# Ten dense pieces in the first filled step, six in the last: a shift by two in a fused two-layer kernel

## The chip, the cores and the metric

The kernel runs on one core of a Trainium2 chip. The metric is the device time of one execution in microseconds (us); less is better. The time before is 886.98 us, the median of three runs (885.87 to 887.53).

## The reference

The reference is two transformer layers on x (32 entries of 64 tokens, 512 features, fp32), each with a condition vector per entry.

```python
# first layer
h = rms(x) * (ln1_w * (1 + cond @ ln1_tw.T))
q, k, v = rope(h @ Wq.T), rope(h @ Wk.T), h @ Wv.T       # 8 heads of 64, one k/v head
x = x + softmax(q @ k.T / 8) @ v @ Wo.T
h = rms(x) * (ln2_w * (1 + cond @ ln2_tw.T))
x = x + (silu(h @ Wg.T) * (h @ Wu.T)) @ Wd.T             # 2048 inner features
# second layer
h = layernorm(x) * (1 + scale(cond)) + shift(cond)
q, c = h @ Wq.T, h @ Wkd.T                                # 16 heads of 32, 4 k/v heads
k, v = c @ Wku.T, c @ Wvu.T
x = x + softmax(mask(rope(q) @ rope(k).T / sqrt(32))) @ v @ Wo.T
```

Attention runs over the 64 tokens of an entry.

## The kernel before, in words

The 2048 tokens are 16 tiles of 128 (two entries each). All matmuls that need fp32 accuracy are made of three: each operand is split into a high part (a cast) and a low part (the difference), and `three` (lines 642 to 645) adds high x high, low x high and high x low. So a weight chunk needs a cast on ScalarE (`guh`, `wdh`) and a subtraction on GpSimd (`gul`, `wdl`) after its DMA.

**The dense part** (gate, up, silu, down of the first layer) is cut into 64 groups: 16 groups of 128 inner features for each of 4 blocks of 512 tokens. Group n has on TensorE (`mlp`, lines 798 to 825) the pieces gate(n), first pair of down(n-1), up(n), second pair of down(n-1). Gate and up are 12 matmuls of 512 columns each, into banks BG and BU; a down pair is two tiles of 3 matmuls, into the two banks BD. Group 0 has two pieces, two come at the end: 256 in all. Every engine has a generator with the same number of pieces (`fill`, line 40, takes the next `count`):

- ScalarE (1698): with gate, silu into `sg` and `wdh`(n); with up, `ah`(n), the cast of `af`; with the second pair, `guh`(n+2) (in group 1 this stands for group 0 too).
- VectorE (1254): with the first pair, two additions of down banks to `xres` (`add_down`, 1252), which free the banks; with up, `af` = up x silu (1265); with the second pair, an addition, `al`(n) = af - ah (1247), an addition.
- GpSimd (518): with gate, `wdl`(n) (516); with the second pair, `gul`(n+2) (511).

TensorE's waits within the pieces: gate(n) for `gul`(n) and for silu(n-1); up(n) for `af`(n-1); a down pair of n for `al`(n), `wdl`(n) and, tile by tile, for the addition that freed its bank (`down`, 786 to 796, the wait at 793).

**The attention part** goes tile by tile, one tile a step, and dense pieces fill TensorE's time. Steps s = 1 to 15 are the first layer's attention, u = -1 to 15 the second's. The order of each engine is written out by hand; the tables `FILL0` and `FILL1` (lines 20, 21) say how many pieces stand at each place of a step. In steps 5 to 15 TensorE does: scores(s), qkv(s+1), fill f1, projection(s-1), fill f2, context(s), fill f3 (lines 1002 to 1028). In u = 0 to 8: scores1(u), f1, qkv1(u+1), projection, f2, f3, context1(u), f4, f5 (1029 to 1062). u = 9 (TAIL) has f1, then qkv1(10), one piece, the transposes of the probabilities, one piece; u = -1 has f1, qkv1(0), projection, f2, f4.

The places of the other engines in steps 6 to 15:

- VectorE (1448 to 1498): softmax_sub(s), turn_x2 of the tile that is made ready for the dense part (steps 6 to 9 and 11 to 14, u = -1 to 2), softmax_norm (it waits for exp), turn_probs, rope_mul(s+1), f1, add_x, turn_queries, f2, low_ctx, scale_h2, f3. In u: softmax_sub1, turn_x2, stats1, two pieces of f1, sums, scaling, turn_probs1, the rest of f1, rope_mul1, and so on.
- ScalarE (1846 to 1889): exp(s), values(s+1), f1, f2, high_ctx, high_h2, square2, high_h, f3, square, norm2 of the next tile (1667; it waits for GpSimd's power). In u also the scale and shift of y (1748), between f4 and f5.
- GpSimd (578 to 611): rstd, rope_sum, f1, f2, low_h2, low_h, f3, rstd2 of the next tile (478).

**Turning through memory.** From step 5 the probabilities (`tp`) are transposed in 32 x 32 blocks on VectorE, written to device memory and read back as `pT` (`probs_away`, `probs_back`, lines 308 to 317); x2, y and the queries go the same way. These DMAs and the loads of the dense weights are all issued by the SP queue, in order, and SP waits in order (397 to 452): in a step x2_away, load_down(n), load_gate_up(n+1), probs_away, x2_back, probs_back, queries_away, queries_back, load_down(n+1), load_gate_up(n+2), load_down(n+2), load_gate_up(n+3), with n = 2 in step 5 and 3 more in each step. load_down(n) waits for `wdl`(n-2) (280), load_gate_up(n) for `gul`(n-2) (274). The context matmuls wait for `pT` (749).

Of the kernel before, what the change touches and what calls it, by code (L numbers as in the profile page):

```python
# [16 lines left out]

FILL0 = {s: (4, 4, 4) for s in range(5, 16)}  # L20
FILL1 = {-1: (4, 4, 0, 4, 0), **{u: (4, 2, 2, 2, 2) for u in range(0, 9)}, 9: (2, 0, 0, 0, 0)}

HEAD, TAIL = 4, 9

# [20 lines left out]
def build(nc, x, xT, pos, condT, ln1_w, ln1_twT, ln2_w, ln2_twT, WqkvT, WoT, gu, WdT,  # L45
# [21 lines left out]
    with ExitStack() as ctx:  # L67
# [153 lines left out]
        def in_layer(t):  # L221
            return 0 <= t < NT
# [237 lines left out]
        def _(pool):  # L460
# [117 lines left out]
            for s in range(1, NT):  # L578
                f1, f2, f3 = FILL0.get(s, (0, 0, 0))
                ready, soon = PREP0.get(s), PREP0.get(s + 1) if s < NT - 1 else PREP1[-1]  # L580
# [31 lines left out]
            for u in range(-1, NT):  # L612
                f1, f2, f3, f4, f5 = FILL1.get(u, (0,) * 5)
                ready, soon = PREP1.get(u), PREP1.get(u + 1)
# [26 lines left out]
        def _(pe):  # L641
# [78 lines left out]
            def scores(t):  # L720
                if t < TURN_Q0:
                    pe.wait_ge(a_qT, t + 1)
                    pe.wait_ge(a_kT, t + 1)
                else:
                    pe.wait_ge(ld_q0, 16 * (t - TURN_Q0 + 1))
                if t > HEAD + 1:
                    pe.wait_ge(a_ch, t)
                    pe.wait_ge(a_cl, t)
                    pe.wait_ge(a_x, t - 1)
                for j in range(KT):  # L730
                    for b in range(2):
                        for i in range(2):
                            r, q = slice(HD0 * i, HD0 * (i + 1)), slice(S * b, S * (b + 1))
                            mm = pe.matmul(ps[q, XB[2 + i], S * j:S * (j + 1)], qkT[r, j, q], qkT[r, KT, q],
                                           start=True, stop=True)
                mm.then_inc(a_sc, 1)
# [265 lines left out]
            for s in range(1, NT):  # L1002
                f1, f2, f3 = FILL0.get(s, (0, 0, 0))
                scores(s)
# [24 lines left out]
            for u in range(-1, NT + 1):  # L1029
                f1, f2, f3, f4, f5 = FILL1.get(u, (0,) * 5)  # L1030
                if in_layer(u):
# [33 lines left out]
        def _(dve):  # L1065
# [382 lines left out]
            for s in range(1, NT):  # L1448
                f1, f2, f3 = FILL0.get(s, (0, 0, 0))
                ready, soon = PREP0.get(s), PREP0.get(s + 1) if s < NT - 1 else PREP1[-1]  # L1450
# [48 lines left out]
            for u in range(-1, NT - 1):  # L1499
                f1, f2, f3, f4, f5 = FILL1.get(u, (0,) * 5)  # L1500
                ready, soon = PREP1.get(u), PREP1.get(u + 1)
# [69 lines left out]
        def _(act):  # L1571
# [274 lines left out]
            for s in range(1, NT):  # L1846
                f1, f2, f3 = FILL0.get(s, (0, 0, 0))
                ready, soon = PREP0.get(s), PREP0.get(s + 1) if s < NT - 1 else PREP1[-1]
# [41 lines left out]
            for u in range(-1, NT - 1):  # L1890
                f1, f2, f3, f4, f5 = FILL1.get(u, (0,) * 5)
                ready, soon = PREP1.get(u), PREP1.get(u + 1)
# [91 lines left out]
```

## Time and profile before

| what | value |
|---|---|
| median of three runs | 886.98 us (885.87 to 887.53) |
| profiled execution | 887.57 us |
| its span (first to last instruction) | 885.7 us |
| TensorE matmuls busy | 852.0 us (96%) |
| TensorE weight loads busy | 707.2 us (80%), beside the matmuls |
| VectorE busy | 631.7 us (71%) |
| ScalarE busy | 447.2 us (50%) |
| GpSimd busy | 406.6 us (46%) |
| mean granted TensorE clock | 0.988 of full |

Busy time is the sum of the instructions of an engine. TensorE is the fullest by far, so a time that TensorE stands idle is paid in full, while idle time of another engine costs only where TensorE waits for it. Times in rows of the timeline are microseconds from the span's start. PE is TensorE, DVE VectorE, ACT ScalarE, POOL GpSimd, SP the queue that issues DMAs.

### The profile page before, as it was taken

The numbers are of one execution on the slowest core, as the hardware profiler recorded it, in microseconds if no ns is written. First come the engines' busy times: TensorE is split into PE (matmuls) and PEld (weight loads), VectorE is DVE, ScalarE is ACT, GpSimd is POOL, SyncE is SP. The second block draws the span as 40 slices with busy tenths as digits, with TensorE's granted clock in tenths as the row PEclk, the third lists the DMA queues.
The fourth block names the chain that finished last, engine by engine and source line by source line (L and its number), as shares of the span: only waits on it lengthen the run. The fifth ranks groups of instructions, "written<-read, shape, count | busy, mean of one in ns | idle before, by whom it ended". The sixth has DMA issues, their size and how long they took to land.

```text
span 885.7 us, 15530 instructions
## 1 busy us (share of the span) xinstructions
PE 852.0 (96%) x5864; PEld 707.2 (80%) x5864; DVE 631.7 (71%) x1005; ACT 447.2 (50%) x821; POOL 406.6 (46%) x304
## 2 busy tenths in 40 slices
PE   9798999999999999999989899999999999999997
PEld 6686888788788888787878678788888888888885
DVE  6686577677666677677546877887877867868886
ACT  4665444544444444445445564563553654644662
POOL 2456445545545545537444644544534534431331
PEclk9899999999999999999999899999999999999999
DMA  9811535435425435334423446355354354330001
GB/s 348 330 32 37 172 99 159 124 110 160 122 87 168 122 104 154 116 99 151 156 96 90 169 122 185 115 166 156 121 164 139 114 175 142 117 102 13 25 27 36
DMA packets 114298, 113.54 MB, mean 128 GB/s; under 512 B 57520, under 2 KB 80048, under 8 KB 114224
## 3 DMA queue, kind: packets, MB, share of 16 engines
q1 hardware_dynamic: 113504, 112.45, 39.8%
q8 instruction: 47, 0.77, 0.4%
q10 hardware_dynamic: 720, 0.09, 0.1%
q14 instruction: 27, 0.22, 0.1%
HBM read 88.15 MB, written 24.38 MB: 127 GB/s over the span
## 4 chain that ended last, share of the span: by engine, by line
PE 65%; DVE 11%; ACT 9%; issue 8%; POOL 6%; POOLq 0%; DVEq 0%; ACTq 0%
PE ps L643 20%; PE ps L645 19%; PE ps L644 19%; PE ps L757 2%; POOL gul L511 2%; ACT yf L1763 1%; PE ps L918 1%; ACT L1643 1%; POOL wdl L516 1%; DVE al L1247 1%; DVE ex L1232 1%; PE ps L689 1%; DVE af L1265 1%; ACT ah L1710 1%; ACT guh L1688 1%
## 5 line engine op out<-in xcount | busy, mean ns | idle before, releaser
L511 POOL TENSOR_TENSOR gul<-rgu,guh 128x1024 fp32r<-128x1024 f32 x64 | 154.3, 2411 | 217.5 <-ACT guh L1688 217.5
L1252 DVE TENSOR_TENSOR xres<-ps,xres 128x512 f32<-128x512 f32 x256 | 174.3, 687 | 67.3 <-PE ps L645 67.3
L643 PE MATMUL ps<-h2h,guh 128*128 128x512 f32 x512 | 205.0, 400 | 2.1 <-issue 2.1
L645 PE MATMUL ps<-h2l,guh 128*128 128x512 f32 x512 | 200.6, 392 | 0.0
L644 PE MATMUL ps<-h2h,gul 128*128 128x512 f32 x512 | 200.2, 391 | 0.0
L643 PE MATMUL ps<-wdh,ah 128*128 128x512 f32 x256 | 102.3, 399 | 14.7 <-DVE al L1247 14.7
L643 PEld LDWEIGHTS ps<-h2h,guh 128*128 128x128 f32 x512 | 96.5, 189 | 23.1 <-issue 2.5
L645 PEld LDWEIGHTS ps<-h2l,guh 128*128 128x128 f32 x512 | 96.5, 188 | 21.1
L1710 ACT CAST ah<-af 128x512 fp32r<-128x512 f32 x64 | 39.8, 621 | 143.8 <-DVE af L1265 138.2
L644 PEld LDWEIGHTS ps<-h2h,gul 128*128 128x128 f32 x512 | 96.5, 189 | 19.6
L644 PE MATMUL ps<-wdh,al 128*128 128x512 f32 x256 | 100.7, 393 | 0.0
L645 PE MATMUL ps<-wdl,ah 128*128 128x512 f32 x256 | 100.7, 393 | 0.0
L516 POOL TENSOR_TENSOR wdl<-rwd,wdh 128x512 fp32r<-128x512 f32 x64 | 82.5, 1289 | 13.4 <-ACT wdh L1696 13.3
L1265 DVE TENSOR_TENSOR af<-ps,sg 128x512 f32<-128x512 f32 x64 | 44.2, 690 | 48.5 <-issue 25.2
L643 PEld LDWEIGHTS ps<-wdh,ah 128*128 128x128 f32 x256 | 48.5, 189 | 30.0 <-DVE al L1247 20.2
L1688 ACT CAST guh<-rgu 128x1024 fp32r<-128x1024 f32 x64 | 66.9, 1045 | 0.0
L1702 ACT ACTIVATE sg<-ps 128x512 f32<-128x512 f32 x64 | 38.2, 597 | 55.4 <-PE ps L645 55.2
L467 POOL TENSOR_TENSOR stat<-stat,minus_half 128x1 f32<-128x1 f32 x48 | 38.3, 798 | 42.2 <-DVE stat L1133 40.9
L645 PEld LDWEIGHTS ps<-wdl,ah 128*128 128x128 f32 x256 | 48.6, 190 | 10.3
L644 PEld LDWEIGHTS ps<-wdh,al 128*128 128x128 f32 x256 | 48.7, 190 | 9.3
L1247 DVE TENSOR_TENSOR al<-af,ah 128x512 fp32r<-128x512 f32 x64 | 48.1, 752 | 9.8 <-ACT ah L1710 6.0
L549 POOL TENSOR_TENSOR qkr<-u 128x128 f32<-128x128 f32 x16 | 11.9, 745 | 80.7 <-DVE u L1317 80.7
(180 smaller groups left out, 1655.5 us busy)
## 6 DMA issues: line engine op xcount, KB each, us to landing
rgu<-gu SPq DMA_DIRECT2D x64, 512.0 KB, 3.9
rwd<-WdT SPq DMA_DIRECT2D x64, 256.0 KB, 3.7
turned_q<-tq SPq DMA_DIRECT2D x20, 320.0 KB, 2.3
qkT<-turned_q SPq DMA_DIRECT2D x20, 320.0 KB, 3.7
turned_p<-tp SPq DMA_DIRECT2D x9, 512.0 KB, 2.6
pT<-turned_p SPq DMA_DIRECT2D x9, 512.0 KB, 3.8
xt<-xT SPq DMA_DIRECT2D x16, 256.0 KB, 2.7
out<-xres SPq DMA_DIRECT2D x15, 256.0 KB, 4.1
```

The source lines that it names most:

```text
L467: pool.tensor_tensor(col, col, minus_half[:, :], ALU.pow).then_inc(signal, 1)
L511: pool.tensor_tensor(gul[i][:, :], rgu[i][:, :], guh[i][:, :], ALU.subtract).then_inc(m_gul, 1)
L516: pool.tensor_tensor(wdl[i][:, :], rwd[i][:, :], wdh[i][:, :], ALU.subtract).then_inc(m_wdl, 1)
L643: pe.matmul(dst, lh, rh, start=start, stop=False)
L644: pe.matmul(dst, ll, rh, start=False, stop=False)
L645: return pe.matmul(dst, lh, rl, start=False, stop=stop)
L1247: dve.tensor_tensor(al[n % 2][:, :], af[:, :], ah[n % 2][:, :], ALU.subtract).then_inc(m_al, 1)
L1252: dve.tensor_tensor(at, bank(BD[i % 2]), at, ALU.add).then_inc(m_x, 1)
L1265: dve.tensor_tensor(af[:, :], bank(BU), sg[:, :], ALU.mult).then_inc(m_af, 1)
L1688: act.copy(guh[i][:, :], rgu[i][:, :]).then_inc(m_guh, 1)
L1702: act.activation(sg[:, :], bank(BG), ACT.Silu).then_inc(m_sg, 1)
L1710: act.copy(ah[n % 2][:, :], af[:, :]).then_inc(m_ah, 1)
```

## The change

Two numbers of the tables change. In step 5 the first fill has two pieces in place of four, so ten in the step in place of twelve; in u = 9 the first fill has four in place of two, so that with the two single pieces of that step there are six in place of four. All engines read these tables. Nothing else is changed.

```diff
-FILL0 = {s: (4, 4, 4) for s in range(5, 16)}
-FILL1 = {-1: (4, 4, 0, 4, 0), **{u: (4, 2, 2, 2, 2) for u in range(0, 9)}, 9: (2, 0, 0, 0, 0)}
+FILL0 = {5: (2, 4, 4), **{s: (4, 4, 4) for s in range(6, 16)}}
+FILL1 = {-1: (4, 4, 0, 4, 0), **{u: (4, 2, 2, 2, 2) for u in range(0, 9)}, 9: (4, 0, 0, 0, 0)}
```

## Rows read from the trace of the kernel before

**Rows 1.** TensorE's waits over the span: us in total, times, longest.
```profile
PE ps L643 <- DVE al L1247: 14.7, 13, 3.9
```

**Rows 2.** Timeline of TensorE: start, duration, instruction, [idle before <- releaser].
```profile
123.96 0.50 PE L643 MATMUL ps<-wdh,ah 128*128 128x512 f32 x1 [0.22 <-DVE al L1247]
...
190.54 0.50 PE L643 MATMUL ps<-wdh,ah 128*128 128x512 f32 x1 [0.39 <-DVE al L1247]
...
420.49 0.50 PE L643 MATMUL ps<-wdh,ah 128*128 128x512 f32 x1 [1.74 <-DVE al L1247]
...
453.87 0.79 PE L643 MATMUL ps<-wdh,ah 128*128 128x512 f32 x1 [3.18 <-DVE al L1247]
...
492.14 0.80 PE L643 MATMUL ps<-wdh,ah 128*128 128x512 f32 x1 [3.93 <-DVE al L1247]
...
527.71 0.50 PE L643 MATMUL ps<-wdh,ah 128*128 128x512 f32 x1 [1.51 <-DVE al L1247]
...
799.32 0.41 PE L643 MATMUL ps<-wqh,yh 128*128 128x384 f32 x1 [0.99 <-issue]
```

**Rows 3.** Timeline of TensorE in the last fill of step 7: matmuls 3 and 31.
```profile
171.06 0.40 PE L645 MATMUL ps<-h2l,guh 128*128 128x512 f32 x1
...
177.44 0.39 PE L643 MATMUL ps<-wdh,ah 128*128 128x512 f32 x1
```

**Rows 4.** Timeline of VectorE: first fills of five steps; 197.85 is a second fill.
```profile
188.05 0.68 DVE L1265 TENSOR_TENSOR af<-ps,sg 128x512 f32<-128x512 f32 x1
188.65 0.68 DVE L1252 TENSOR_TENSOR xres<-ps,xres 128x512 f32<-128x512 f32 x1
...
197.85 0.69 DVE L1265 TENSOR_TENSOR af<-ps,sg 128x512 f32<-128x512 f32 x1 [0.92 <-issue]
...
418.19 0.69 DVE L1265 TENSOR_TENSOR af<-ps,sg 128x512 f32<-128x512 f32 x1
...
451.75 0.69 DVE L1265 TENSOR_TENSOR af<-ps,sg 128x512 f32<-128x512 f32 x1
...
489.47 0.69 DVE L1265 TENSOR_TENSOR af<-ps,sg 128x512 f32<-128x512 f32 x1
...
525.59 0.69 DVE L1265 TENSOR_TENSOR af<-ps,sg 128x512 f32<-128x512 f32 x1
```

**Rows 5.** Timeline of GpSimd around the end of step 7 and in step 8.
```profile
176.64 2.41 POOL L511 TENSOR_TENSOR gul<-rgu,guh 128x1024 fp32r<-128x1024 f32 x1 [0.57 <-ACT guh L1688]
179.00 1.29 POOL L516 TENSOR_TENSOR wdl<-rwd,wdh 128x512 fp32r<-128x512 f32 x1
...
200.22 2.40 POOL L511 TENSOR_TENSOR gul<-rgu,guh 128x1024 fp32r<-128x1024 f32 x1 [5.73 <-ACT guh L1688]
```

**Rows 6.** Timeline of ScalarE: step 8 (three rows), and the end of step 15.
```profile
187.84 1.28 ACT L1631 ACTIVATE bdv<-ps,stat 64x64 f32<-64x64 f32 x4 [4.34 <-DVE t L1190]
...
190.72 1.28 ACT L1702 ACT_TABLE_LOAD   x1
...
192.52 0.61 ACT L1696 CAST wdh<-rwd 128x512 fp32r<-128x512 f32 x1
...
443.57 2.77 ACT L1763 ACTIVATE yf<-yt,sh_ada,sc_ada 128x64 f32<-128x64 f32 x8
```

**Rows 7.** Timeline of the SP queue in step 8.
```profile
186.33 0.33 SPq L285 DMA_DIRECT2D turned_p<-tp  x1
...
188.46 0.37 SPq L289 DMA_DIRECT2D pT<-turned_p  x1
```

**Rows 8.** The SP queue in step 5; rwd and rgu go out at 91.14 and 91.51.
```profile
91.99 0.43 SPq L285 DMA_DIRECT2D turned_p<-tp  x1
96.47 0.38 SPq L289 DMA_DIRECT2D pT<-turned_p  x1
```

**Rows 9.** The page's DMA issues: count, KB each, median us to landing.
```profile
pT<-turned_p SPq DMA_DIRECT2D x11, 256.0 KB, 2.7
```

**Rows 10.** Timeline of TensorE's weight loads: context of step 8.
```profile
202.81 0.85 PEld L757 LDWEIGHTS ps<-pT,bdv 128*128 128x128 f32 x4
```

## The prediction

> **What bounds the kernel now.** The page first: TensorE is busy nearly all of the span, so the question is what it waits for. TensorE's waits have one large entry: the first matmul of a down pair waits for `al` from VectorE, 14.7 us in 13 waits [rows 1]. The timeline says where: in the first fill of steps 6 to 9 and 11 to 14, then in step 15 and u = -1, 0, 1, 2 [rows 2], where 123.96 stands for steps 6 and 11, 190.54 for the six others and 527.71 also for u = 2, which has the same 1.51. From u = 3 to u = 8 there is none, and one more wait of 0.99 stands ahead of qkv1(10) [rows 2]. Matmuls of 512 columns start every 0.228 us: the 3rd of a last fill stands at 171.06, the 31st at 177.44 [rows 3]. So a gate or up piece (12 matmuls) is 2.73 us and a down pair (6) is 1.37.
>
> **What the change does to the order.** A group n has four pieces: gate(n), first down pair of n-1, up(n), second down pair of n-1; only group 0 has two. Step 5 issues 10 pieces in place of 12, so every later fill of four is two pieces behind in the list. Until now a fill was up, second pair, gate, first pair; it becomes gate, first pair, up, second pair. The work is the same, and step 9 of the second layer gets the two pieces back. The change is thus a turn of the phase in some 50 fills, and each wait has to be looked at again.
>
> **Part 1, the thirteen waits.** In a first fill VectorE comes late, since softmax and rope stand ahead. Now it does `af`, an addition, then `al` (with ScalarE's `ah` between), and TensorE starts when `al` is there: 190.54 - 188.05 = 2.49 us after VectorE takes up the fill [rows 2, 4]. After the change the first pair of the fill uses an `al` that is long done, and it is the second pair, at the same place in TensorE's order (30 matmuls in), that waits: its bank is freed by the first addition of the fill, 0.68 us [rows 4] plus 0.06 for the signal. TensorE can go on 1.75 us earlier relative to VectorE.
> But VectorE arrives later. At a step's end GpSimd runs `gul`, then the power for the next rstd, and ScalarE's norm2, its exp and VectorE's softmax sums follow in line. `gul` starts 2.37 us after `af` (197.85 to 200.22) [rows 4, 5]. With up third in the fill and not first, up ends 18 matmuls = 4.10 us later: in step 7 at 177.44, where the last pair starts now [rows 3]. So `af` comes at 177.65, `gul` from 180.0 to 182.4, then the power. Now `gul` (176.64) and `wdl` (179.00, 1.29 us) let the power start at 180.29 [rows 5]. VectorE is 2.1 us later. Net, each of six steps loses 2.1 - 1.75 = 0.35. Steps 6 and 11 had 0.17 less of a gap, as nothing of tile preparation stood before `gul`; they lose 0.7. Sum: 6 x 0.35 + 2 x 0.7 = **+3.5 us**.
> Step 15: VectorE arrives as before (both orders have the four low-weight subtractions, `gul` and `wdl` ahead on GpSimd). 420.49 - 418.19 = 2.30 becomes 0.74 [rows 2, 4]: **-1.55**. In u = -1 ScalarE's scale and shift of y, now at 443.57 [rows 6], comes behind `ah` and the weight cast, so 1.28 later, and what follows to VectorE with it; 453.87 - 451.75 = 2.12 becomes 0.74: -1.38 + 1.28 = **-0.1**. In u = 0 the same, 492.14 - 489.47 = 2.67: **-0.65**. In u = 1 and 2, 527.71 - 525.59 = 2.12 becomes 0.74, and VectorE is 0.42 later (one addition more behind the last pair): **-0.95 each** [rows 2, 4]. Together -4.2.
> The bounds of Part 1 are: all thirteen gaps go, with the restart of about 0.25 us each, 14.7 + 3.3 = -18; or a gap of every step grows by the 2.1 us and nothing is given back, 8 x 2.1 = +17 with the five others unchanged. I take -0.7, between them, as each piece of it has its own row.
>
> **Part 2, the probabilities' way through memory.** The SP queue runs load_down(n), load_gate_up(n+1), probs_away, x2_back, probs_back in this order in each step (n is here the group whose load stands at the step's head). load_down(n) waits for `wdl` of group n-2. That gate piece was in the last fill of the step before; it is now the first piece of this step, and ScalarE reaches it behind exp and values. So probs_away, now issued at 186.33 [rows 7], waits. Worked out: values start at 187.84 + 2.1 = 189.94, take 1.28, the table load 1.28, silu until the cast 0.52 (190.72 + 1.28 to 192.52), the cast 0.61, `wdl` 1.29 and 0.1 of signals: the load is issued at 195.0 [rows 5, 6]. The store goes out 0.85 later, behind 768 KB. A step shows just that: in step 5 the store of 91.99 landed at 96.47, 4.5 us, against 188.46 - 186.33 = 2.1 when alone [rows 7, 8]. The load back then lands 2.7 later [rows 9]: 195.0 + 0.85 + 4.5 + 2.7 = 203.1. The context matmuls want it when their weight load starts, 202.81 + 0.35 = 203.2 [rows 10]. The 11.6 us of cover of now (188.46 + 2.7 against 202.81) are used up, the wait is about 0.1 in each of eight steps: **+1**. Bounds: none, or 1.5 us late in each, +12, if this chain is that much longer; nothing in it can gain. In step 5 context comes two pieces (4.10 us) earlier, at 99.2, and its data at 96.47 + 2.7 = 99.2 [rows 8, 9]: 0 to +0.5, taken as 0.
> On this the Trainium skill ("DMA: Bandwidth & Descriptors", section on queues, rings and completion order) says that descriptors of a queue are consumed in ring order on each DMA engine, and that a semaphore lands only after the earlier writes of that engine. By that rule the store cannot pass the two loads; the 4.5 us of step 5 agree. Were it to pass them, Part 2 would be 0.
>
> The steps of the second layer turn too, but their load_down is issued before the probabilities are ready, so nothing is late there; y's way out and back moves some 4 us later and lands as ScalarE wants it. I take 0, bounds 0 to +3.
>
> **Part 3, the end.** u = 9 has four pieces in place of two before qkv1(10), which needs `af` of the last group (now 0.99 us late [rows 2]). Scores start 4.1 us earlier, but with the new order the softmax sums and scaling stand between the two additions and the last `af`, and it comes at 799.9 + 0.1 = 800.0 on the old clock against 799.32: **+0.7**. Bounds: -1.1 (wait gone) to +2.
>
> **Sum.** +3.5 - 4.2 + 1.0 + 0.7 = +1.0 us. The profiled execution took 887.57 (span 885.7), so the changed one would take 888.6; the median before, 886.98, is 0.6 below it, so the forecast is **888.0 us**. About 0.2% (1.8 us) is what a measurement of this kernel can tell from no change, and this is less.
>
> **Rivals.** Slower: the loads back are late. Its place is the context matmul of steps 6 to 9 and 11 to 14, its price the landing less 203.2. For it speaks that no slack is left by the rows; against it, that step 5's landing just fits. It decides from 0.1 us of lateness on; at 1 us in each of eight steps the time is 888.0 + 7 = 895. Chance 0.35.
> Faster: the waits for `al` go, and VectorE is not later, because norm2 is not what softmax waits for. For it speaks that the consumer of `al` moves a whole fill away; against it the chain by `gul`. With Part 1 at 8 x -0.65 - 5.7, so -11 in place of -0.7, it is 888.0 - 10.2 = 878; half of it gives 883. Chance 0.25.
> That the change does not do what it says is out: the counts sum to 256 pieces in both.
> After the long wait of u = -1 a matmul takes 0.79 us in place of 0.39, and after that of u = 0 0.80 [rows 2]: TensorE is at the lower of its two clocks for some microseconds. As both waits stay by the sum, nothing is counted for that; in the faster case it would add to the gain.
>
> **Numbers.** Forecast (within 0.2%) 0.40, the slower rival 0.35, the faster 0.25. The range takes the slower case to 8 x 0.9 us and the faster one to half: 882.0 to 895.0 us. The likeliest case's own range is 885.5 to 889.5.
>
> **What would show it.** Waits of TensorE for `al` gone or nearly so, and in their place waits of about 0.9 us for L1252 (the addition) in steps 6 to 9 and 11 to 14; GpSimd's power in those steps about 2 us later than now against the scores; SP's load of rwd 16 us after the scores and the store of `tp` right behind it, 4 to 5 us to landing; context's wait under 0.5. The forecast is wrong if context waits 1 us or more, if the first fill of a step shows no wait, or if the steps from u = 3 on begin to wait.

## The result, and the profile after

The changed kernel takes **892.65 us** (median of 4 executions, 891.78 to 893.43) against 886.81 for the kernel before on the same chip (885.87 to 887.53): a ratio of 1.0075, 95% interval 1.0049 to 1.0101. It is slower by 5.8 us. The profiled execution took 892.86 us, its span is 891.0 against 885.7.

TensorE's waits over the span in the changed kernel (us in total, times, longest), the answer to [rows 1]:

```profile
PE ps L643 <- DVE xres L1252: 15.0, 13, 3.0
PE ps L643 <- issue: 4.5, 3, 2.1
PE ps L757 <- DMA pT<-turned_p: 3.1, 5, 1.3
```

The 14.7 us of waits for `al` are gone but for one of 0.71, and 15.0 us of waits for the addition of line 1252 stand in their place. New are five waits of the context matmuls (line 757) for `pT`. The timeline of TensorE places them; the answer to [rows 2]:

```profile
98.84 1.13 PE L757 MATMUL ps<-pT,bdv 128*128 128x256 f32 x4 [0.83 <-DMA pT<-turned_p]
...
133.09 1.13 PE L757 MATMUL ps<-pT,bdv 128*128 128x256 f32 x4 [0.21 <-DMA pT<-turned_p]
154.51 0.47 PE L643 MATMUL ps<-wdh,ah 128*128 128x512 f32 x1 [0.91 <-DVE xres L1252]
168.36 1.13 PE L757 MATMUL ps<-pT,bdv 128*128 128x256 f32 x4 [1.28 <-DMA pT<-turned_p]
189.76 0.47 PE L643 MATMUL ps<-wdh,ah 128*128 128x512 f32 x1 [0.91 <-DVE xres L1252]
202.96 1.13 PE L757 MATMUL ps<-pT,bdv 128*128 128x256 f32 x4 [0.61 <-DMA pT<-turned_p]
237.12 1.13 PE L757 MATMUL ps<-pT,bdv 128*128 128x256 f32 x4 [0.15 <-DMA pT<-turned_p]
...
418.70 0.47 PE L643 MATMUL ps<-wdh,ah 128*128 128x512 f32 x1 [0.95 <-issue]
423.42 0.47 PE L643 MATMUL ps<-wdh,ah 128*128 128x512 f32 x1 [0.38 <-DVE xres L1252]
456.64 0.47 PE L643 MATMUL ps<-wdh,ah 128*128 128x512 f32 x1 [3.04 <-DVE xres L1252]
484.01 0.91 PE L895 MATMUL ps<-qkT 32*64 32x64 f32 x64 [0.82 <-DMA qkT<-turned_q]
494.29 0.47 PE L643 MATMUL ps<-wdh,ah 128*128 128x512 f32 x1 [2.32 <-DVE xres L1252]
523.80 0.50 PE L643 MATMUL ps<-wdh,ah 128*128 128x512 f32 x1 [0.71 <-DVE al L1247]
529.53 0.47 PE L643 MATMUL ps<-wdh,ah 128*128 128x512 f32 x1 [1.36 <-DVE xres L1252]
564.26 0.47 PE L643 MATMUL ps<-wdh,ah 128*128 128x512 f32 x1 [0.62 <-DVE xres L1252]
804.60 0.41 PE L643 MATMUL ps<-wqh,yh 128*128 128x384 f32 x1 [1.47 <-issue]
```

The wait of 0.91 stands in all eight steps 6 to 9 and 11 to 14; two of the eight are shown. The lengths of the steps, from the starts of the scores matmuls (first layer line 734, second line 895), after less before:

| stretch | forecast | measured |
|---|---|---|
| up to step 5 | 0 | +0.2 |
| step 5, less the two pieces (4.10) | 0 | -0.5 |
| steps 6 to 14 | +3.5 and +1.0 | +7.45 |
| step 15 and u = -1 | -1.65 | +0.7 |
| u = 0 | -0.65 | -2.8 |
| u = 1 | -0.95 | +0.8 |
| u = 2 | -0.95 | -0.9 |
| u = 3 to 8 | 0 | -0.1 |
| u = 9, less the two pieces, and the end | +0.7 | +0.4 |
| sum | +1.0 | +5.3 |

Steps 12 to 14, with nothing but the wait of 0.91, last 33.73 to 33.79 us (33.25 to 33.30 before); step 10, without any wait, lasts 32.58 in both kernels. A context wait adds itself and 0.2 to 0.3 us: step 7 lasts 35.25, 1.97 more than before, of which 1.28 is its wait.

Two rows hold the granted clock of the profiled executions too. In the trace before, it is 0.66 from 85 to 90 us, behind a wait of 2.08; in the trace after it is 1.00 there, behind the same wait. The code up to there is the same, so this is luck. Of the ten traces of the experiments below, which have that wait too (2.06 to 2.08), the clock falls behind it in seven and stays full in three. A step 5 of ten pieces lasts 35.0 to 35.1 us in those where it falls and 33.4 in e3, where it stays full and nothing waits. So luck gives the changed kernel some 1.6 us back in step 5, and hides its 0.83 us of waiting for `pT`. From 490 to 500 us, in u = 0, the clock is 0.66 before and 0.83 after. This is worth 1.1 us: e8 has the tables of before there and the same wait of 3.93, and at 0.83 its u = 0 lasts 36.89 against 37.99.

**VectorE's chain in step 8** (VectorE, then GpSimd, then ScalarE; the answer to [rows 4, 5, 6]):

```profile
182.47 1.09 DVE L1165 STREAM_TRANSPOSE tx<-xn 128x512 f32<-128x512 f32 x1 [2.07 <-ACT xn L1668]
183.49 0.11 DVE L1133 TENSOR_SCALAR stat<-stat 128x1 f32<-128x1 f32 x1
184.42 0.69 DVE L1227 TENSOR_REDUCE smx<-ex 128x8 f32<-128x512 f32 x1 [0.81 <-ACT ex L1643]
...
188.94 1.28 DVE L1252 TENSOR_TENSOR xres<-ps,xres 128x512 f32<-128x512 f32 x2
```

```profile
178.78 2.39 POOL L511 TENSOR_TENSOR gul<-rgu,guh 128x1024 fp32r<-128x1024 f32 x1 [2.74 <-ACT guh L1688]
181.13 0.55 POOL L467 TENSOR_TENSOR stat<-stat,minus_half 128x1 f32<-128x1 f32 x1
```

The same power in the kernel before, where the scores start at 178.90:

```profile
180.24 0.56 POOL L467 TENSOR_TENSOR stat<-stat,minus_half 128x1 f32<-128x1 f32 x1
```

ScalarE in the changed kernel:

```profile
181.72 0.73 ACT L1668 ACTIVATE xn<-xres,stat 128x512 f32<-128x512 f32 x1 [2.39 <-POOL stat L467]
182.46 1.28 ACT L1643 ACT_TABLE_LOAD   x1
183.75 0.63 ACT L1643 ACTIVATE ex<-ex 128x512 f32<-128x512 f32 x1
```

Read upwards from the wait: TensorE starts at 189.76 when the first addition (188.94 + 0.68) has freed a bank; that addition stands behind rope, sums and the transpose `tx`, which waits 2.07 us for ScalarE's norm2; norm2 waits 2.39 us for GpSimd's power; the power stands behind `gul` of the last fill. Scores of step 8 start at 177.60 here and at 178.90 before, so VectorE takes up the fill 11.34 us behind them in place of 9.15 [rows 4]: 2.2 us later. The power is late by as much: it starts 3.53 us behind the scores in place of 1.34.

**The SP queue in step 8**, the answer to [rows 7]:

```profile
193.96 0.33 SPq L281 DMA_DIRECT2D rwd<-WdT  x1
194.33 0.43 SPq L275 DMA_DIRECT2D rgu<-gu  x1
194.81 0.43 SPq L285 DMA_DIRECT2D turned_p<-tp  x1
195.34 0.38 SPq L289 DMA_DIRECT2D x2t<-turned_x  x1
199.11 0.37 SPq L289 DMA_DIRECT2D pT<-turned_p  x1
```

The store of `tp` goes out 17.2 us behind the scores, against 7.4 before, and lands 4.3 us later, against 2.1.

### The profile page after: what moved, and what is told of

It reads as the page before. It is cut to its first block, busy times and chain, and to the rows that moved or that the text cites. A ratio compares the mean times of both kernels' runs of the same rounds, so it can differ in the third digit from the quotient of the medians.

```text
span 891.0 us, 15532 instructions
## 1 busy us (share of the span) xinstructions
PE 851.2 (96%) x5864; PEld 704.9 (79%) x5864; DVE 634.9 (71%) x1005; ACT 449.5 (50%) x823; POOL 406.0 (46%) x304
## 4 chain that ended last, share of the span: by engine, by line
PE 65%; ACT 7%; DVE 7%; issue 7%; DMA 6%; POOL 6%; SPq 1%; POOLq 0%; DVEq 0%; ACTq 0%
PE ps L643 20%; PE ps L645 19%; PE ps L644 19%; DMA turned_p<-tp 3%; PE ps L757 2%; DMA pT<-turned_p 2%; ACT yf L1763 1%; POOL gul L511 1%; POOL wdl L516 1%; PE ps L918 1%; DMA turned_y<-ty 1%; PE ps L689 1%; PE ps L680 1%; DVE xres L1252 1%; ACT guh L1688 1%
## 5 line engine op out<-in xcount | busy, mean ns | idle before, releaser
L1252 DVE TENSOR_TENSOR xres<-ps,xres 128x512 f32<-128x512 f32 x256 | 172.9, 686 | 50.2 <-PE ps L645 50.2
L516 POOL TENSOR_TENSOR wdl<-rwd,wdh 128x512 fp32r<-128x512 f32 x64 | 84.3, 1317 | 113.3 <-ACT wdh L1696 113.3
L1247 DVE TENSOR_TENSOR al<-af,ah 128x512 fp32r<-128x512 f32 x64 | 51.6, 806 | 7.1 <-ACT ah L1710 2.6
L467 POOL TENSOR_TENSOR stat<-stat,minus_half 128x1 f32<-128x1 f32 x48 | 35.2, 733 | 43.0 <-DVE stat L1133 39.3
L643 PE MATMUL ps<-wqh,yh 128*128 128x384 f32 x128 | 45.1, 352 | 1.5 <-issue 1.5
```

The lines of the kernel that those rows point to most:

```text
L467: pool.tensor_tensor(col, col, minus_half[:, :], ALU.pow).then_inc(signal, 1)
L516: pool.tensor_tensor(wdl[i][:, :], rwd[i][:, :], wdh[i][:, :], ALU.subtract).then_inc(m_wdl, 1)
L643: pe.matmul(dst, lh, rh, start=start, stop=False)
L1247: dve.tensor_tensor(al[n % 2][:, :], af[:, :], ah[n % 2][:, :], ALU.subtract).then_inc(m_al, 1)
L1252: dve.tensor_tensor(at, bank(BD[i % 2]), at, ALU.add).then_inc(m_x, 1)
```

## The experiments

**The first layer's part and the second's.** Two kernels cut the change in two: e1 turns the pieces in the first layer and turns them back at the end of step 15; e2 leaves the first layer and turns them from the end of step 15 on.

The tables of e1, against before:

```diff
+FILL0 = {5: (2, 4, 4), **{s: (4, 4, 4) for s in range(6, 15)}, 15: (4, 4, 6)}
 FILL1 = {-1: (4, 4, 0, 4, 0), **{u: (4, 2, 2, 2, 2) for u in range(0, 9)}, 9: (2, 0, 0, 0, 0)}
```

and of e2:

```diff
+FILL0 = {**{s: (4, 4, 4) for s in range(5, 15)}, 15: (4, 4, 2)}
+FILL1 = {-1: (4, 4, 0, 4, 0), **{u: (4, 2, 2, 2, 2) for u in range(0, 9)}, 9: (4, 0, 0, 0, 0)}
```

> The shift by two in the first layer alone (step 15 gives the two pieces back, u = -1 to 9 as before). Theory A (the loss is made in steps 5 to 9 and 11 to 14, by additions that wait behind the late softmax and by late loads of the probabilities; the second layer gives something back): 6 to 8 us over the kernel before, so 893 to 895 us, more than the full change, with waits of about 0.9 us for L1252 in eight steps and of pT in four or five contexts. Theory B (the loss comes from the end, u = 9, or is spread over all steps): 887 to 889 us.

> The shift by two in the second layer alone (step 15 has ten pieces, u = 9 six; steps 5 to 14 as before). Theory A: the first layer's waits are those of the kernel before (about 0.4 us each), the long wait of u = 0 is not followed by matmuls at the lower clock, and the time is 1 to 3 us under the kernel before, 884 to 886 us. Theory B: 2 to 4 us over it, 889 to 891 us.

Measured: e1 891.79 us (889.61 to 892.46), ratio to before 1.0060 (1.0047 to 1.0074); e2 887.27 (885.79 to 890.47), ratio 1.0022 (1.0008 to 1.0036); before 885.95 (17 executions). e1's waits:

```profile
PE ps L643 <- DVE al L1247: 10.1, 4, 3.9
PE ps L643 <- DVE xres L1252: 7.7, 9, 0.9
```

The waits for the addition are those of the first layer, and the four for `al` in u = -1 to 2 are back. Three context matmuls wait (0.48, 0.30 and 0.29 us, in steps 6, 9 and 11), not the same ones as in the changed kernel, though steps 5 to 14 have the same tables. In e1's trace the loss against before is 4.9 us at the first scores1 and stays there to the end. So the first layer carries most of the loss, though less than theory A had (893 to 895 us).

e2 lies between its two theories. The second layer costs 0.2% in the median, where the prediction's terms from u = -1 on, with the end, come to a gain of 1.95 us. The place of that cost is not shown: e2's profiled execution, at a mean granted clock of 0.992, is 1.3 us shorter than that of before (span 884.4 against 885.7). Its five executions at 0.992 took 885.8 to 887.5 us, its seven at 0.987 and 0.988 took 887.0 to 890.5.

**The context waits.** e3 is the changed kernel with the probabilities' store and load back ahead of the two weight loads on the SP queue.

```diff
+                probs_away(s)
+                if moved:
+                    x2_back(ready)
+                probs_back(s)
                 load_down(n)
                 load_gate_up(n + 1)
-                probs_away(s)
-                if moved:
-                    x2_back(ready)
-                probs_back(s)
```

> The full change, with load_down(n) and load_gate_up(n+1) issued behind probs_back in the SP queue in the first layer. Theory A: the store of tp goes out 7 to 9 us earlier and lands after 2 to 3 us; the context waits of steps 5 to 9 (3.1 us of gap, some 3.5 with restarts) go: 3 to 4 us less than the full change, 888.5 to 890 us; the waits of 0.9 us for the addition stay. Theory C (contention: the memory is slow in those steps whatever the order, or the loads now come late for the last fill): 892 us or more.

Step 7 on its SP queue:

```profile
149.95 0.33 SPq L285 DMA_DIRECT2D turned_p<-tp  x1
150.38 0.38 SPq L289 DMA_DIRECT2D x2t<-turned_x  x1
152.06 0.37 SPq L289 DMA_DIRECT2D pT<-turned_p  x1
156.69 0.34 SPq L281 DMA_DIRECT2D rwd<-WdT  x1
```

The store lands in 2.1 us and no context matmul of steps 5 to 14 waits. All steps with the wait of 0.91 last 33.72 to 33.76. Steps 6 to 14 together take 302.5 us, against 298.55 in the kernel before and 306.0 in the changed one. So of the 7.45 us lost there, 3.95 are the waits for the addition and 3.5 the context waits. Step 15 starts 5.0 us earlier than in the changed kernel, of which 0.4 stood before step 5; the profiled execution is 4.0 us shorter (span 887.0 against 891.0). But the median is 892.11 us (888.87 to 893.31; ratio 1.0064, 1.0046 to 1.0081). The two executions with a mean granted clock of 0.992 took 888.9 us, the four with 0.987 and 0.988 took 892.1 to 893.3. So the profiled execution comes out as theory A has it, and the median where theory C has it. At equal clock the context waits cost what the trace says; the other four executions ran at a lower clock, and nothing shows where in them or why.

**The power ahead of the last fill.** e4 is the changed kernel with GpSimd's power for the next tile moved from behind the last fill of a step to ahead of it, in steps 5 to 14. The value it needs is there by then. e6 does the same to the kernel before.

```diff
+                if s > HEAD and s < NT - 1 and soon is not None:
+                    rstd2(soon)
                 fill(pieces, f3)
                 if s == NT - 1:
                     low_y(0)
-                if s > HEAD and soon is not None:
                     rstd2(soon)
```

> The full change, with GpSimd's power for norm2 ahead of the last fill's gul in steps 5 to 14. Theory A (gul, power, norm2, exp is the chain that makes VectorE late): norm2, exp and rope come 2 us earlier, the eight waits of 0.9 us for the addition go, and as values, silu and wdl come earlier too, so do load_down and the probabilities: the context waits go with them. 8 x 1.1 + 3.5, so 10 to 13 us less than the full change, 880 to 883 us. Theory D (VectorE is late by its own work in this order, one addition more behind the last pair and softmax behind it): 0 to 2 us less, 890.5 to 892.5 us.

> The kernel before with the same reordering as e4: GpSimd takes the power for the next tile's scale ahead of the last fill. Theory A (the chain gul, power, norm2, exp, softmax sums is what makes VectorE late in the first fill, in either phase of the pieces): the eight waits for al in steps 6 to 9 and 11 to 14 go (0.22 in two, about 0.6 in six, each with its restart), the five others stay; 886 - 4 to 5 = 881 to 882 us, beside e4's 880.5. So without this chain the turned table costs nothing. Rival B (the chain is late only because the turn brings up to the end of the fill): before keeps its eight waits and stays at 885 to 887 us.

Measured: e4 **880.52** us (879.67 to 881.83), ratio 0.9936 (0.9923 to 0.9949). e6 **880.19** (878.64 to 880.57), ratio 0.9918 (0.9904 to 0.9932), before 887.50 in its comparison. The added line moves all later line numbers by one. GpSimd, ScalarE and VectorE of e4 around the same step's scores (172.70):

```profile
171.06 0.56 POOL L467 TENSOR_TENSOR stat<-stat,minus_half 128x1 f32<-128x1 f32 x1
171.58 1.30 POOL L516 TENSOR_TENSOR wdl<-rwd,wdh 128x512 fp32r<-128x512 f32 x1
173.88 2.40 POOL L511 TENSOR_TENSOR gul<-rgu,guh 128x1024 fp32r<-128x1024 f32 x1 [1.00 <-ACT guh L1689]
```

```profile
174.33 0.71 ACT L1669 ACTIVATE xn<-xres,stat 128x512 f32<-128x512 f32 x1
```

```profile
175.42 1.10 DVE L1166 STREAM_TRANSPOSE tx<-xn 128x512 f32<-128x512 f32 x1
...
181.54 1.28 DVE L1253 TENSOR_TENSOR xres<-ps,xres 128x512 f32<-128x512 f32 x2
```

norm2 waits for nothing, and VectorE takes up the fill 8.84 us behind the scores in place of 11.34. TensorE's waits in e4:

```profile
PE ps L644 <- DVE xres L1253: 7.8, 5, 3.0
```

All eight waits of steps 6 to 9 and 11 to 14 are gone, and the context waits with them: the whole attention chain stands 2.5 us earlier in its step, and so does the store of `tp`. Every step from 6 to 14 lasts 32.58. The sum closes: these steps took 306.0 us and take 293.2, 12.8 less, and the medians differ by 12.1. In e6 too every step from 6 to 14 lasts 32.58, and its waits for `al` are down from 13 to 5 (11.9 us).

So e4 and e6, which differ only in the tables, have the same length in each of steps 6 to 14. Their medians differ by 0.3 us; measured against the executions of before beside each, e4 is 0.2% longer (0.9936 and 0.9918). In steps 6 to 14 the tables cost nothing of themselves: what they cost was 2.2 us more of lateness in one chain, and that chain need not be there in either.

**The same in step 15 and the second layer.** e7 is e4 with the chain brought forward there too; e10 is e7 with the tables of before.

On GpSimd:

```diff
-                if s > HEAD and s < NT - 1 and soon is not None:
+                if s > HEAD and soon is not None:
                     rstd2(soon)
                 fill(pieces, f3)
                 if s == NT - 1:
                     low_y(0)
-                    rstd2(soon)
...
+                if soon is not None:
+                    rstd2(soon)
                 if in_layer(u + 2):
                     low_y(u + 2)
                 if ready is not None:
                     low_h2(ready)
-                if soon is not None:
-                    rstd2(soon)
```

On VectorE mean_sq2(soon) stands ahead of scale_h2(ready) in u, and on ScalarE norm2(soon) ahead of scale_shift_y(0) in step 15. In u on ScalarE:

```diff
+                if soon is not None:
+                    square2(soon)
                 if u < TAIL:
                     scale_shift_y(u + 2)
                     high_y(u + 2)
                 if ready is not None:
                     high_h2(ready)
                 if soon is not None:
-                    square2(soon)
+                    norm2(soon)
                 if u == -1:
                     high_w1_out()
                 fill(pieces, f5)
-                if soon is not None:
-                    norm2(soon)
```

> e4, and the same chain brought forward in step 15 and in the steps of the second layer: GpSimd's power ahead of the fill and of low_y, ScalarE's square and norm2 ahead of the scale and shift of y where they can be, VectorE's mean ahead of the scaling of the tile. Theory A: the waits of TensorE for L1252 in u = -1 and u = 0 (3.04 and 2.55 us in e4) fall to under 1 each, the clock does not fall behind them in any execution, and runs agree more closely: 875 to 877 us against 880.5. Rival B (VectorE's own queue of softmax, transpose and sums in those steps is what ends last, not the power): the two waits keep over 1.5 us each, 879 to 881 us.

> The reordering of e7 with the table of before. Theory A (with the chain ahead of the fill, the phase of the pieces is nearly free): 874 to 877 us beside e7's 875.4; the waits for al in u = -1 and 0 (3.18 and 3.93 us in e6) fall to 1 to 2 each, as al needs 1.75 us more of VectorE and ScalarE behind the same arrival than the addition does, so up to 2 us above e7. Rival B (the phase of before is worth something of its own, as the step-15 and GpSimd queues are free there): under 873.

Measured: e7 875.38 us (874.34 to 879.06), ratio 0.9876 (0.9857 to 0.9895). The waits for L1252 of u = -1 and u = 0, 3.04 and 2.55 us in e4, are 0 and 0.81. A new one of 2.38 stands ahead of context1(0), for `pT`. The executions do not agree more closely, as theory A wanted: they spread over 4.7 us, at mean clocks of 0.990 to 0.996. e10: **873.36 us** (871.98 to 873.88), ratio 0.9849 (0.9834 to 0.9865), the fastest of all. It has two waits for `al` left:

```profile
PE ps L643 <- DVE al L1247: 5.0, 2, 3.2
```

The wait in u = -1 is gone; that of u = 0 stays at 3.24, where theory A had 1 to 2. Its steps 6 to 14 last 32.58 as e7's do. So with this chain out of the way the tables of before are no worse, as theory A had it, and by the medians 2.0 us better (nor is the time below 873, as rival B wanted); the two intervals of the ratios touch. The wait for `pT` is not what makes the difference: u = 0 lasts 36.71 in e7 with it and 37.42 in e10, where the wait of 3.24 stands in its place. In the traces e10 is shorter in u = 1 and 2 (1.5 us), where e7 waits 0.77 and 0.72 for the addition and e10 for nothing, in step 15 and u = -1 (0.3), and in u = 9 less its two pieces (0.4).

**The wait for `pT` in u = 0.** e11 is e7 with the probabilities' store and load back ahead of the weight loads in u = 0 alone.

```diff
                 if u < TAIL:
+                    if u == 0:
+                        probs_away1(u)
+                        probs_back1(u)
                     load_down(n)
                     load_gate_up(n + 1)
                     if ready is not None:
                         x2_back(ready)
-                    if u >= 0:
+                    if u > 0:
```

> e7, and in u = 0 alone SP issues the store and the load back of the probabilities ahead of the weight loads, which wait there for a wdl that GpSimd does behind 6.04 us of low-weight subtractions (e7: wdl at 478.76, the store issued at 481.42, the load back landing at 491, 2.38 us late for the context matmuls). Theory A: that wait goes, 875.4 becomes 873. Rival B (the loads of weights and of the turned tile that now come later are late instead, or the clock moves by as much): 875 or more.

Measured: 876.59 us (876.09 to 878.09), ratio 0.9893 (0.9875 to 0.9911). The wait is gone, and scores1(0) to scores1(1) takes 33.37 in place of 36.71; scores1(1) to (2) takes 36.64 in place of 34.95, so half is given back, to waits for the queries' load back (0.69), for `al` (0.85) and a longer one for the addition (1.33). No gain shows in the times, whose spread overlaps e7's, as rival B had it. In the profiled executions the stretch from scores1(0) to the end is 1.4 us shorter than e7's, and the stretch before it, whose code is the same, 3.4 us longer: 1.9 ahead of step 5, and 1.3 in step 5 by the clock. So a gain of 1.4 us is in one trace, and no measured time shows it.

**The size of step 5, and the end.** e8 is before with ten pieces in step 5 but fourteen in step 6, so that the turn lasts one step. e9 is before with two pieces moved from the last fill of u = 8 to u = 9.

The line of e8 that differs from before, and that of e9:

```diff
+FILL0 = {**{s: (4, 4, 4) for s in range(7, 16)}, 5: (2, 4, 4), 6: (6, 4, 4)}
...
+FILL1 = {-1: (4, 4, 0, 4, 0), **{u: (4, 2, 2, 2, 2) for u in range(0, 8)}, 8: (4, 2, 2, 2, 0), 9: (4, 0, 0, 0, 0)}
```

> Before, with ten pieces in step 5 but fourteen in step 6 (six in its first fill), so that from step 6's second fill on the pieces stand in the phase of before; the end is before's. Theory A (what costs is the turn of the phase in the later steps, not that step 5 has fewer pieces): 885.5 to 887.5 us, the waits for al as before. Rival B (the loss lies in step 5 or in what follows it at once, a context wait or a clock step): 888 us or more, with the loss standing by step 7.

> Before, with two pieces moved from the last fill of u = 8 to the first of u = 9; the first layer and u = -1 to 7 are before's. Theory A (the longer u = 9 costs what the trace of the change shows there, +0.43): 886 to 887 us, 0 to +1 against before. Rival B (the end costs the 2 us of the upper bound, or u = 8 opens a wait): 888 us.

Measured: e8 887.09 us (11 executions, 886.72 to 888.26), ratio 1.0003 (0.9994 to 1.0011): theory A; the time does not change when the turn lasts one step. In e8's trace steps 5 and 6 are 1.6 us longer than before (waits of 0.91 for the addition and 0.67 for silu in step 6), every step from 7 to 14 lasts as before, and u = 0 is 1.1 us shorter by the clock. e9 890.21 us (12 executions, 887.54 to 893.19), ratio 1.0035 (1.0022 to 1.0048), 2.7 us and not 0 to 1; the second half of rival B, a wait that u = 8 opens, is what the trace shows. It is no picture of the change's end, though. With the last fill of u = 8 gone, scores1(9) come too soon for the queries' load back, and qkv1(10) waits longer:

```profile
790.56 0.91 PE L895 MATMUL ps<-qkT 32*64 32x64 f32 x64 [1.57 <-DMA qkT<-turned_q]
...
801.90 0.41 PE L643 MATMUL ps<-wqh,yh 128*128 128x384 f32 x1 [2.06 <-issue]
```

In the changed kernel that fill is there and scores1(9) wait for nothing. The fill of u = 8 was the cover of that load, and my expectation forgot it. The two waits are 1.57 and 1.07 more than before, which is the 2.6 us by which scores1(10) are later. The rest of the profiled execution's 5.3 us is clock: 0.66 from 880 us to the end.

## Why the prediction came out as it did

The time lies within the range, but at the slower rival's end and 4.6 us above the forecast; the likeliest case was not it. That the range holds it is in part luck: the slower rival was 1 us of lateness in each of eight steps, and what came were four context waits, together with losses in places where the sum had a gain or nothing (3 and 5 below), and some 1.6 us given back by the clock in step 5, which the sum did not have. One of the prediction's own signs of being wrong came true: the context wait of step 7 is 1.28 us.

1. **The turn of the phase and the wait that replaces `al`: right in mechanism and size.** Forecast: eight waits of about 0.9 for L1252 and VectorE 2.1 us later. Measured: eight of 0.91, VectorE 2.2 later. By e3's trace the steps lose 3.95 us by it in all, where Part 1 had 3.5 (0.59 and 0.65 in steps 6 and 11 for 0.7, and 0.42 to 0.50 in the six others for 0.35). Two figures of the prediction do not follow from its own terms: steps 6 and 11 would lose 0.35 + 0.17 = 0.52, not 0.7, and the wait would be 0.39 + 0.35 = 0.74, not about 0.9.
2. **The context waits: right in mechanism, sized too small, 1.0 us for 3.5.** The SP queue's load was forecast 16.1 us behind the scores and came at 16.4 (193.96 less 177.60). The failed term is the landing of the store behind the two loads, "4.5 us against 2.1 when alone", one number from the one row of step 5 for all steps [rows 8]. In the changed kernel it is 4.8, 5.8, 4.3 and 4.7 in steps 6 to 9, 4.2 to 4.4 in steps 11 to 14, and 5.2 in step 5. The mean of the eight is 4.6, so 4.5 was a fair mean; but a late landing is paid in full and an early one gives nothing back. The context matmuls start 3.0 us behind the issue of the load back, as counted (2.7 + 0.35), but for step 8 with 3.85: there the load back is late and not the store. Four waits of 0.21, 1.28, 0.61 and 0.15 follow, 2.25 us, and 3.5 with the restarts and a small rest, where Part 2 had 1.0 for eight of 0.1. Steps 11 to 14 have none. The size is that of one execution: e1, with the same tables in these steps, has waits of 1.07 in three steps and takes 2.4 us more than e3. The sum left 0.1 us of slack against a number known from one row. It also left out that Part 1 moves the context back, to 24.6 us behind the scores from 24.1, which is in its favour.
   The wait of 0.83 in step 5, taken as 0, stands at full clock only. In e1, e4 and e8, where the clock falls there, context starts 25.8 us behind the scores and waits for nothing; in e3, at full clock, it starts at 24.2. The prediction had read its 99.2 from a trace in which the clock had fallen.
   By the rule that the prediction draws on from the Trainium skill ("DMA: Bandwidth & Descriptors", queues, rings and completion order), descriptors of a queue are consumed in ring order on each DMA engine. The traces agree with that: the store lands in 2.1 us with nothing right ahead of it (e3, step 7) and in 4.2 to 5.8 behind the 768 KB. It gives the order, not the size.
3. **Step 15 and u = -1: -1.65 forecast, +0.7 measured.** Two waits were not in the sum; that of u = -1 itself came out as forecast (3.04, for 3.18 less 0.1). In step 15 the first pair now stands ahead of where it was, and it needs `wdl`, which GpSimd does at 417.33 behind 5.58 us of low-weight subtractions (line 560): 0.95. "VectorE arrives as before" was true and not enough, as the piece waits for GpSimd also. And scores1(0) wait 0.82 for the queries' load back.
4. **u = 0: -0.65 forecast, -2.8 measured.** The wait went from 3.93 to 2.32, where the prediction's terms give 3.28. But scores1(0) had already waited 0.82 in front of it (3), and the two make 3.14. Taken together the size was right, and 0.8 us of it stands one row of the table higher. The rest is the clock of 490 to 500 us (0.66 and 0.83), 1.1 us.
5. **y's way through memory: 0 forecast, it is late.** In u = 1 ScalarE waits 1.89 us for `yt`:

```profile
514.40 0.61 ACT L1696 CAST wdh<-rwd 128x512 fp32r<-128x512 f32 x1
516.90 2.76 ACT L1763 ACTIVATE yf<-yt,sh_ada,sc_ada 128x64 f32<-128x64 f32 x8 [1.89 <-DMA yt<-turned_y]
```

and VectorE behind it for ScalarE:

```profile
521.50 0.15 DVE L1138 TENSOR_SCALAR stat<-stat 128x1 f32<-128x1 f32 x1 [4.50 <-ACT xn L1663]
```

   y's store goes out at 508.19 behind two weight loads and its load back is issued at 513.93, 5.7 us later; in the kernel before it was 4.5 (503.35 and 507.86), and ScalarE took up the scale and shift only at 515.17. Here it is free for it at 515.01, 3.9 us sooner behind scores1(0). VectorE's `af` (521.67) and ScalarE's `ah` (522.40) come behind that, and TensorE waits 0.71 for `al` and then 1.36 for the addition. So u = 1 is 0.8 longer and not 0.95 shorter: 1.75 us, inside the bounds of 0 to +3 that stood beside the 0. u = 2, where `yt` is in time, came out at the forecast -0.9.
6. **The end: +0.7 forecast, +0.4 measured.** The wait for `af` went from 0.99 to 1.47 in the place named.
7. **The faster rival** is out: VectorE is later, and norm2 is what it waits for (2.07 us at `tx`). e4 and e6 show by taking it away that this chain is the whole cause of the waits of steps 6 to 14, in both phases; those of step 15 stay. The prediction had read that chain and used it for 2.1 us of lateness, but not asked what of the 14.7 us of before it explains: 5.3 us in steps 6 to 14 (298.55 to 293.2). For its own faster case, "8 x -0.65 - 5.7", it gives no working of the 5.7.

So three of the misses are the same: the turn moves a piece, and a store, a load or a low weight whose lateness had been covered is not covered any more. They are worth 2.5 (context), 2.3 (step 15 and u = -1) and 1.75 (u = 1); u = 0 gives 2.1 back.

## What to carry to other kernels

When a table turns the phase of two interleaved pipelines, list for every piece that moves ahead all that it waits for (here `al`, the bank, `wdl`, `pT`, `yt`, `qkT`), and give each its own slack; the one that was last before tells nothing of the next. Where the slack of a transfer comes out near zero, its landing time from one row is not enough: put the spread of all rows of that transfer behind other traffic into the sum. And look for a small instruction behind large ones in an in-order queue: a power of 0.55 us, issued ahead of the 3.7 us of subtractions that it did not depend on, was worth 12 us in the changed kernel, twice the effect of the change under study, and 7 us in the kernel before.

## What the runs showed of the hardware that was not expected

- The same store of 256 KB took 2.1 us from issue to landing with no load right ahead of it (all of steps 6 to 14 of e3) and 4.2 to 5.8 us right behind two loads of 768 KB together (the changed kernel), in steps with the same order of issue. The spread of 1.6 us is larger than the slack of 0.1 that was counted on.
- The granted clock fell behind a wait of TensorE in some executions and not in others with the same code up to there: at 85 to 90 us, behind 2.1 us of waiting, 0.66 in the trace before and 1.00 in the trace after. Of all twelve traces it fell in eight and stayed full in four. Matmuls of 512 columns then start 0.43 us apart in place of 0.23 for some 3 us, the lower of the clock's two levels (1.2 and 2.4 GHz), and the step is 1.6 us longer. e3 took 888.9 us at a mean of 0.992 and 892.1 to 893.3 at 0.987 and 0.988, and e2 shows such a difference too. e9's last 11 us ran at 0.66. The start of step 5, with the same code ahead of it, stood at 72.2 to 75.5 us in the twelve traces. An edit that saves 3 to 4 us can so be hidden from a median, and its profile has to be read step by step.
